# A two-layer cross-attention kernel on one core: the norms' reciprocal root moves from GpSimd to ScalarE, with table loads called for ahead and VectorE's bias products behind the rows

## What is computed

```python
def _layer_norm(x, scale, offset):
    mu = jnp.mean(x, axis=-1, keepdims=True)
    var = jnp.var(x, axis=-1, keepdims=True)
    return (x - mu) * jax.lax.rsqrt(var + LN_EPS) * scale + offset

def _cross_attention(q_in, kv_in, wq, bq, wk, bk, wv, bv, wo, bo, bias_k, bias_v):
    qh = (q_in @ wq + bq).reshape(b, q_len, H, K)          # 16 heads of 128
    kh = (kv_in @ wk + bk).reshape(b, t, H, K)             # 1500 keys
    vh = (kv_in @ wv + bv).reshape(b, t, H, K)
    kh = jnp.concatenate([kh, jnp.broadcast_to(bias_k, (b, 1, H, K))], axis=1)
    vh = jnp.concatenate([vh, jnp.broadcast_to(bias_v, (b, 1, H, K))], axis=1)
    logits = jnp.einsum('bqhk,bthk->bhqt', qh, kh) / scale
    weights = jax.nn.softmax(logits, axis=-1)
    ctx = jnp.einsum('bhqt,bthk->bqhk', weights, vh).reshape(b, q_len, H * K)
    return ctx @ wo + bo

x = x + _cross_attention(_layer_norm(x, ...), ctx, ...)    # layer 1
x = x + _cross_attention(_layer_norm(x, ...), ctx, ...)    # layer 2
h = _layer_norm(x, ln_mlp_scale, ln_mlp_offset)
return x + jax.nn.gelu(h @ w_fc1 + b_fc1, approximate=False) @ w_fc2 + b_fc2
```

## Time and profile before

| | us |
|---|---|
| median of three runs | 1203.68 |
| lowest and highest | 1203.36, 1203.79 |
| the profiled execution, its own time | 1203.09 |
| its span | 1201.3 |

### The profile page before, as it was taken

How to read it: one execution, slowest core, us unless ns; L and a number is a source line. 1 busy time by engine, 2 the same in 40 slices (tenths; PEclk the granted TensorE clock), 3 DMA queues, 4 the chain that set the end, 5 groups by cost and what they waited for, 6 DMA issues and landing times.

```text
span 1201.3 us, 26535 instructions
## 1 busy us (share of the span) xinstructions
PE 1186.7 (99%) x7688; PEld 1101.6 (92%) x7688; DVE 884.2 (74%) x1584; ACT 764.2 (64%) x1501; POOL 875.0 (73%) x744
## 2 busy tenths in 40 slices
PE   8999999999999999999999999999999999999998
PEld 7788999999999999998997899999999999999898
DVE  6876878787778787776776877777777777777754
ACT  5756666666666666676584666666666666667755
POOL 5847878787878787677552779696968787867762
PEclk9999999999999999999999999999999999999999
DMA  5411222222222222233230122222222222312331
GB/s 163 140 30 52 59 77 59 74 60 73 60 73 63 70 66 67 58 64 99 87 96 19 40 58 71 65 73 62 73 61 75 60 79 56 82 42 66 78 95 40
DMA packets 148297, 83.61 MB, mean 70 GB/s; under 512 B 121180, under 2 KB 122604, under 8 KB 148248
## 3 DMA queue, kind: packets, MB, share of 16 engines
q1 hardware_dynamic: 147704, 82.27, 26.5%
q10 hardware_dynamic: 544, 0.75, 0.2%
HBM read 68.56 MB, written 0.53 MB: 58 GB/s over the span
## 4 chain that ended last, share of the span: by engine, by line
PE 90%; DVE 2%; POOL 2%; issue 2%; ACT 2%; DMA 1%; POOLq 0%; DVEq 0%; SPq 0%; ACTq 0%
PE psum L796 39%; PE psum L803 13%; PE psum L804 12%; PE psum L805 12%; PE psum L762 5%; PE psum L848 4%; PE psum L783 2%; PE psum L712 1%; POOL pt L624 1%; DMA w_raw<-weights 1%; POOL w L550 1%; PE psum L728 0%; PE psum L827 0%; DVE g_prod L1290 0%; DVE qh L1325 0%
## 5 line engine op out<-in xcount | busy, mean ns | idle before, releaser
L624 POOL TENSOR_TENSOR pt<-slots,pt 125x512 fp32r<-125x512 f32 (+3 forms) x384 | 452.5, 1187 | 162.2 <-ACT slots L1073 156.4
L796 PE MATMUL psum<-qs,ctx 128*125 128x384 f32 (+1 forms) x2304 | 528.1, 367 | 0.8 <-ACT slots L1092 0.8
L796 PEld LDWEIGHTS psum<-qs,ctx 128*125 128x125 f32 x2304 | 396.9, 186 | 42.5 <-ACT slots L1092 1.9
L803 PE MATMUL psum<-ctx,pt 125*128 125x258 f32 (+1 forms) x1344 | 381.5, 284 | 2.4 <-POOL pt L624 2.1
L804 PE MATMUL psum<-ctx,pt 125*128 125x256 f32 (+1 forms) x1344 | 379.4, 282 | 0.0
L805 PE MATMUL psum<-ctx,pt 125*128 125x258 f32 (+1 forms) x1344 | 378.9, 282 | 0.0
L1072 ACT ACTIVATE pt<-slots 125x512 fp32r<-125x512 f32 (+3 forms) x384 | 221.1, 576 | 212.0 <-DVE slots L1373 207.2
L1389 DVE TENSOR_TENSOR t_max<-psum,t_max 125x512 f32<-125x512 f32 (+1 forms) x282 | 175.2, 621 | 156.9 <-PE psum L796 155.0
L803 PEld LDWEIGHTS psum<-ctx,pt 125*128 125x128 f32 (+1 forms) x1344 | 253.5, 189 | 15.5 <-POOL pt L624 4.4
L804 PEld LDWEIGHTS psum<-ctx,pt 125*128 125x128 f32 (+1 forms) x1344 | 254.2, 189 | 6.5
L805 PEld LDWEIGHTS psum<-ctx,pt 125*128 125x128 f32 (+1 forms) x1344 | 254.8, 190 | 0.0
(11 more groups left out here) (108 smaller groups left out, 1023.0 us busy)
## 6 DMA issues: line engine op xcount, KB each, us to landing
nat_stage<-ctx_nat SPq DMA_DIRECT2D x60, 375.0 KB
tr_stage<-ctx_tr SPq DMA_DIRECT2D x60, 375.0 KB, 3.1
w_raw<-weights SPq DMA_DIRECT2D x70, 256.0 KB, 2.7
qt<-turn SPq DMA_DIRECT2D x256, 32.0 KB, 2.0
qt<-turn SPq DMA_DIRECT2D x224, 24.0 KB, 1.9
dk_rest<-dk_rows SPq DMA_DIRECT2D x6, 256.0 KB, 3.7
w_raw<-weights ACTq DMA_DIRECT2D x2, 256.0 KB, 5.3
dk_first<-dk_rows SPq DMA_DIRECT2D x2, 256.0 KB, 3.7
```

Of the source, the lines that this page charges most:

```text
L624: nc.gpsimd.tensor_tensor(split_weights(h, LO, c), logits(h, c), as_f32(split_weights(h, HI, c)), ALU.subtract).then_inc(pt_lo, 1)
L796: last = mm(scores(h, k), ctx_tr_chunk(half, a, c), qs[h][:, m, half, 0:R], start=(half, a, m) == terms[0], stop=(half, a, m) == terms[-1])
L803: mm(out_bank[:, 0:D + 2], hi, ctx_nat_hi(c), start=(c == 0), stop=False, skip_group_check=True)
```

## The change

Three things are changed.

The power on GpSimd is replaced by ScalarE's `Abs_reciprocal_sqrt`, with the epsilon as a bias from a small tile `eps` (`root(m)`). It waits for the last aggregate and not for `ln_v`. The Newton step stays on VectorE.

ScalarE's table then has to be switched. A one-column instruction on `act_ready` calls for the new table ahead of its use: for the root at the start and in each layer's last output quad, for Exp in each layer's last query quad, after head 13's copies. The load ahead of the Gelu stays.

`while_waiting()` moves behind VectorE's normalized rows. On ScalarE the copy of the second weight moves behind the first norm's rows, and the copy of the last weight of the third norm behind that norm's rows.

```diff
-            def norm(m):
-
-                pool.wait_ge(ln_chain, INIT + m * LN_CHAIN + 1)
-                settle(pool)
-                nc.gpsimd.tensor_tensor(ln_y[:], ln_v[:], minus_half[:], ALU.pow).then_inc(ln_pow, 1)
-
...
+            def root(m):
+
+                act.wait_ge(ln_aggr, INIT + m * RG + RG)
+                go(ln_y[:], ln_mv[:, :, 1], ACT.Abs_reciprocal_sqrt, bias=eps[:]).then_inc(ln_root, 1)
+
...
-            act.wait_ge(filled, INIT + 1)
-            go(act_ready[:], filler[:, 0:1], ACT.Copy)
+            act.wait_ge(setup_step, INIT + 1)
+            settle(act)
+            go(act_ready[:], eps[:], ACT.Abs_reciprocal_sqrt)
+            root(0)
             for u in range(3):
                 act.wait_ge(w_in[u], 16)
                 go(w[u][:, HI, :], w_raw[u][:], ACT.Copy).then_inc(w_hi, 1)
+                if u == 0:
+                    norm_rows(0)
                 if u == 1:
-                    norm_rows(0)
...
+                        if last_quad and u == 1:
+                            go(act_ready[:], eps[:], ACT.Exp)
...
-                        if not (first_quad and u == 0) and not (last_quad and u == 3 and l + 1 < LAYERS):
+                        if not (first_quad and u == 0) and not (last_quad and u == 3):
                             weight_hi(l * JOBS + quad * 4 + (H + 4 + u), u, l * 8 + quad + 5)
+                        if last_quad and u == 1:
+                            go(act_ready[:], eps[:], ACT.Abs_reciprocal_sqrt)
...
+                root(l + 1)
                 norm_rows(l + 1)
+                if l + 1 == LAYERS:
+                    weight_hi(LAYERS * JOBS + 3, 3, LAYERS * 8)
                 norm(l + 1)
...
-                while_waiting()
-                dve.wait_ge(ln_pow, INIT + m + 1)
+                dve.wait_ge(ln_chain, INIT + base + 1)
+                dve.wait_ge(ln_root, INIT + m + 1)
...
+                while_waiting()
                 if m == 0:
                     dve.wait_ge(tables_in, 16 * N_TABLES)
```

More of the change, by code:

```diff
@@ L130, in build @@
         ln_v = sb("ln_v", [RGP, RG], F32)
-        minus_half = sb("minus_half", [RGP, RG], F32)
+        eps = sb("eps", [RGP, 1], F32)
         ln_y = sb("ln_y", [RGP, RG], F32)
@@ L141, in build @@
         assert place_at[0] - at_turn == GT[0] * D * 4
-        act_ready = sb("act_ready", [P, 1], F32)
+        act_ready = sb("act_ready", [RGP, 1], F32)
         N_TR, N_NAT = DC * 2 * T, NCT * NAT_W
@@ L233, in build @@
         gp_ready, gp_used = sem("gp_ready"), sem("gp_used")
-        ln_stats, ln_aggr, ln_chain, ln_pow = sem("ln_stats"), sem("ln_aggr"), sem("ln_chain"), sem("ln_pow")
+        ln_stats, ln_aggr, ln_chain, ln_root = sem("ln_stats"), sem("ln_aggr"), sem("ln_chain"), sem("ln_root")
         xn_dve, xn_act, xt_mm = sem("xn_dve"), sem("xn_act"), sem("xt_mm")
@@ L271, in build @@
             "pe": [w_used, xt_mm, q_mm, qp_mm, lb_mm, s_mm, pv_mm, ot_mm, pn_picked, oth_used, c_mm, y_mm],
-            "act": [saved, xn_act, w_hi, h_hi, q_hi, qp_out, most_qs_hi, first_qs_hi, copied, exp_done, on_act, ot_out,
+            "act": [saved, ln_root, xn_act, w_hi, h_hi, q_hi, qp_out, most_qs_hi, first_qs_hi, copied, exp_done, on_act, ot_out,
                     p80_hi, oth_early, oth_hi, c_hi, g32_ready],
@@ L277, in build @@
                     oth_lo, c_lo, xb_ready],
-            "pool": [zeroed, setup_step, nat_lo, tr_lo, w_lo, ln_pow, qs_hi, qs_lo, pt_lo, dv80_step, dvm_ready],
+            "pool": [zeroed, setup_step, nat_lo, tr_lo, w_lo, qs_hi, qs_lo, pt_lo, dv80_step, dvm_ready],
         }
@@ L597, in _ @@
             settle(pool)
-            norm(0)
             pool.wait_ge(xn_dve, INIT + RG // 2)
@@ L694, in _ @@
                     weight_lo((l + 1) * JOBS + u, u)
-                norm(l + 1)
                 pool.wait_ge(xn_dve, INIT + (l + 2) * (RG // 2))
```

2 lines of the change are left out of this document (1 added, 1 removed).

## The result

The changed kernel takes 1206.88 us, the median of 15 runs; the kernel before took 1204.57 beside it (15 runs). One run of the changed kernel stood at a mean granted clock of 0.478 and took 2449.53; the other 14 lie between 1205.09 and 1209.28, and the ratio is taken from them. It is 1.0022, with a 95% interval of 1.0015 to 1.0029: about 0.2% slower. In the profiled execution it takes 1206.60 with a span of 1204.8, which is 3.5 over the profiled execution of before. That one, 1203.09, was among the quickest of its kernel, so the profiles overstate the difference: the medians differ by 2.3.

A forecast was written before the change was run, and what follows sets the result against it. TensorE was taken to bound the kernel (90% of the chain), after an opening paced by the input queue. -0.57 + 1.56 + 0.34 + 0.93 = +2.26 on the 1203.68 median gave 1205.9; own range 1205.4 to 1206.7 (+1.7 to +3.0).

The forecast's parts named there:

- Norms: Second and third norm: transposes start 0.29 and 0.28 earlier, no more because filler matmuls bound them; -0.57 us in all.
- The root: First norm: ScalarE's root takes 0.29 us plus 0.03 handover, so VectorE's next step starts at 6.83, 1.17 earlier.
- Queue: Start: dk_rows' store and everything behind SyncE's wait go 1.56 us later, delaying head 4's weight; +1.56 to the loop's end.
- The sign named for it: Layer 0, head 4: its matmuls' wait for GpSimd would show as 2.7 us instead of 1.19.
- Layer 0's load: Exp table load in layer 0's last query quad: VectorE starts 0.71 late, 0.37 is regained; +0.34 us.
- Layer 1's load: Exp table load in layer 1's last query quad: ScalarE's high half of head 15 starts late; +0.93 us.
- Root loads: Table loads before the second and third norms' roots: they fall in ScalarE's idle time and cost nothing.
- Rival 1: Start: the queue's delay is absorbed and the weight lands at 21.1 as now; +0.7, or 1204.4 us; chance 0.18.
- Rival 2: Head 4: idle time grows to 2.75 and TensorE's pace then slows, 2.0 us on top; 1207.9 us; chance 0.10.
- Rival 3: Two visible table loads: each holds ScalarE about twice as long, 1.28 us more at each; 1208.5 us; chance 0.05.
- Rivals 4 and 5: 4: loads and queue hide, only norms count, 1203.1, chance 0.04; 5: filler no bound, norms give 3.3, 1200.4, chance 0.03.

The follow-up runs named there:

- second measurement: The changed kernel measured again, unaltered, beside run 9 on one chip: 1206.75 us, ratio 1.0025 to the kernel before.
- run 6: The changed kernel with 22 filler matmuls in place of 30 ahead of the second and third norms' transposes: 1204.29 us, ratio 1.0009 to the kernel before.
- run 1: The changed kernel with the first norm's bias differences back ahead of VectorE's Newton step: 1205.20 us, ratio 1.0009 to the kernel before.
- run 2: The kernel before with only the first norm's bias differences moved behind the rows, power still on GpSimd: 1207.80 us, ratio 1.0036.
- run 7: The changed kernel with the first nat_stage and tr_stage transfers issued ahead of SyncE's wait for hdiff: 1203.67 us, ratio 0.9995 to the kernel before.
- run 10: Run 9's kernel with SyncE's two weights also ahead of its wait and 22 fillers: 1201.45 us, 0.9976; then with bias differences back in front: 1200.71 us, 0.9976.
- run 5: The changed kernel with the call for Exp's table moved behind ScalarE's last copy of the scaled queries: 1206.13 us, ratio 1.0020 to the kernel before.
- run 9: The changed kernel with nat_stage and tr_stage transfers ahead of SyncE's wait and Exp's call behind the last scaled-query copy: 1202.20 us, ratio 0.9990 to the kernel before.
- run 8: The changed kernel with 14 fillers behind the first blocks and 10 behind the first quad of heads, layer 0: 1207.36 us, ratio 1.0025 to the kernel before.
- run 4: The changed kernel with the first norm's bias differences back in front and no calls for Exp's table ahead: 1206.81 us, ratio 1.0029 to the kernel before.

## Why the prediction was right, and where not

The forecast was 1205.9 and the time is 1206.88; as a difference, 2.26 was forecast and the medians give 2.31, and 2.68 in the second measurement. The whole is right, the parts are less so. The sum's own range is not: the ends named in the text add up to some +0.4 to +3.3, not to +1.7 to +3.0.

- **Norms, -0.57.** Measured -0.38 and -0.37 in both profiles. The idle 0.29 and 0.28 went, and some 0.09 more, because the transposes themselves took 0.77 instead of 0.86 up to the fillers behind them; why is not shown. That the filler bounds the rest is shown by run 6.
- **The root, 0.29, starting VectorE's chain at 6.83.** It took 0.30, and the chain started at 6.93, for a handover of 0.12 to VectorE where 0.03 was taken from GpSimd's.
- **Queue, +1.56.** The mechanism stands (runs 1, 2, 7 and the table of landings). The store was 1.65 later, the weight's copy 1.27 in the first profile and 2.02 in the second, and at head 14 the delay was 2.1 and some 2.8, the lower clock included. The step that was too simple is that the line is as long as it was, only later: its length changes by up to 2 us between executions. The weight's own issue, which was to hardly change, came at 16.36 in the first profile and at 17.99, or 1.46 later, in the second; it did not bind, since tr_stage landed later still. The sign named for it failed in the first profile: head 4's matmuls were to wait 2.7, and they waited 1.03 there, since TensorE itself was late from head 2, and 2.38 in the second.
- **Layer 0's load, +0.34.** From head 14 to head 15 the delay grows by 0.53 (0.71 was forecast), and 0.22 of it is back by the first copy of scores (0.37 forecast). Net 0.31.
- **Layer 1's load, +0.93.** 0.73. The dummy took 0.20, not 0.29, and ScalarE's next step started 0.09 before its end. Between the two profiles the loss at head 15 looks smaller still (+3.40 before the loop, +3.48 behind): the profiled execution of before had a pitch of 2.48 a head there, and the changed one 2.43. Run 2, without a visible load, has the 2.43 too (34.60 for the loop), so this is chance; runs 6 and 10 have 2.48 in their profiles.
- **Layer 1 behind the load, not in the forecast.** From head 15's product to the first matmul of the weighted context it takes 29.02 in the kernel before and in run 2, and 29.32 and 29.30 in the changed kernel, where VectorE starts its first step behind the maxima after 0.49 of idle time. No term stands for this 0.3. The load ahead of head 15 does not make it, since run 5, with the call late, has 29.34; the cause stays open.
- **Root loads, 0.** Right: the loads at 591.59 and 1172.19 lie in idle time.
- **Rival 1**, the queue absorbed: refuted by run 7, which gains where nothing else is changed.
- **Rival 2**, TensorE's pace: given 0.10, by an idle time of 2.75 ahead of head 4 and a slower pace at a clock that reads full. What the profiles show is another thing, a granted clock that reads 0.50, and it comes behind shorter pauses as well (1.79 and 2.38 in the changed kernel). The sum put it at nothing. Under it lies the second load behind SyncE's wait, head 2's weight, whose lateness was not priced. Of the runs of the changed kernel, 24 of 25 have a mean clock under 1.000; of the kernel before, 24 of 83, on three chips. Before's runs at 1.000 average 1203.4 to 1203.8, the others 1204.9 to 1205.3. The difference of the shares, 0.96 - 0.29 = 0.67, times that 1.3 to 1.8 is some 0.9 to 1.2 of the 2.3 to 2.7 (an estimate: the same late weights that lower the clock cost time by themselves, and the two are not separated). A comparison on one chip says the same: at a mean clock of 0.999 the changed kernel takes 1206.35 (5 runs) and the kernel before 1205.01 (8 runs), so of the 2.7 between the medians about half is left. That the lower clock comes with the late weights is shown by run 1 (3 of 11 runs) and run 10 (0 of 21). With head 4's weight alone early it is 7 and 5 of 11 (runs 7 and 9). Run 10 has both of the other weights early and fewer fillers too; fewer fillers alone did not do it (run 6, 8 of 11), but in run 10 their part is not told apart. Run 8, meant to separate clock and lateness, did not.
- **Rival 3**, a load that holds ScalarE twice as long: refuted. The six rows of loads in the changed kernel's profile read 1.28, and the instruction behind starts 0.01 later. The Trainium skill, "ScalarE: Activation LUTs", section "What ACT_TABLE_LOAD costs", adds a drain of 1.38; no row here shows one, and the measurement decides.
- **Rivals 4 and 5** fall with the above: the queue and layer 1's load are visible, and the filler does bound.

So the mechanisms forecast are there, but the sum came out partly by luck, because errors offset each other. The norms gave 0.2 more than forecast and the loads cost 0.2 less; the 0.3 in layer 1 was not foreseen. Norms and loads together with these 0.3 make +0.6, where +0.7 was forecast. What is left of the 2.3 to 2.7, some 1.7 to 2.1, is the queue and the lower clock together, against a queue of +1.56 alone. If the estimate for the clock holds, the queue's own part is only 0.5 to 1.2, and the lower clock, counted at nothing, made up for it. What stays open is the exact split between late weight and lower clock.

## What to carry to other kernels

Before you move a short instruction behind something, list all that the queue of a waiting engine holds behind that wait: here one subtraction of 0.41 us held back two weights and two slow transfers, and the remedy was to issue first what waits for nothing (run 10), not to move the subtraction back. Put a table load where the next instruction of its engine has the longest wait for another engine, and ask who waits for that next instruction; some 4 us apart, the same load cost 0.73 or, by the profile, nothing, and another 25 us on it cost 1.3. A filler sized for a slow chain has to be shortened together with the chain.

## What the runs showed of the hardware

- A transfer into nat_stage with the one into tr_stage behind it, which took 8.0 to 10.6 to land, held up a later weight on the same queue: the weight was copied 0.6 to 0.75 behind tr_stage's landing in ten of ten profiles, 4.6 to 6.0 after its own issue where that was read. With the two transfers out of the way it took 2.6 to 2.8 (runs 9 and 10). The earlier trace rows show a DMA share of 0.33 for a nat_stage load alone. The Trainium skill, "DMA: Bandwidth & Descriptors", section "Why a DMA increments its semaphore by 16 and not by 1", says that the number of engines is the largest one up to 16 that divides the size of the slowest dimension of both access patterns. For 125 partitions that gives 5 of 16, an estimate worked out from this rule. The share read here, 0.33, agrees with its 0.31.
- In all 14 profiles each fall of the granted clock below 1.00 lies between 16 and 34 us, in windows of 2 us, in or behind a pause of TensorE ahead of head 2 or head 4: one of 1.72 (run 4), 1.79 (busy 0.38 of the 2 us before), 1.89 (run 7), 2.20 (run 1), 2.35 (run 8), 2.38 (busy 0.72 of the 2 us in which it ended) and 3.35 (run 2). It stayed at 1.00 behind 1.71 ahead of head 2 in run 8 and behind 2.12 ahead of head 2 in run 2, as behind the 1.19 of the kernel before. So the length of the pause alone does not decide.
- Among the 16 issues of SyncE behind layer 0's attention, which take 0.61 each, one took longer in 13 of the 14 profiles: 0.92 to 1.58, in the kernel before 1.05.
